# First graph layer of a four-layer network: one-hots built by ScalarE, message parts added in TensorE's sums, earlier record loads

## The chip, the cores and the metric

One core of one Trainium2 chip. The metric is the device time of the whole kernel in microseconds (us), the median of several runs. All four layers and their preparation are one program; the change touches the first layer's loop ("the product phase") and a few lines around it.

## What is computed

A node table `x` (6250 nodes x 64) passes through four graph layers over the same 200,000 edges, each followed by an addition and a layer norm. The change is in the first one:

```python
x0, x1 = x[:, :16], x[:, 16:].reshape(-1, 16, 3)          # of the edge's source node
w00, w01, w10, w11 = (silu(edge_attr @ w1 + b1) @ w2 + b2).reshape(-1, 4, 16, 16)
out0 = alpha * (einsum('eu,e,euw->ew', x0, sh0, w00) + einsum('eui,ei,euw->ew', x1, sh1, w11) / SQRT3)
out1 = alpha * (einsum('eu,ei,euw->ewi', x0, sh1, w01) + einsum('eui,e,euw->ewi', x1, sh0, w10)) / SQRT3
msgs = concatenate([out0, out1.reshape(-1, 48)], axis=1)
agg  = segment_sum(msgs, dst)
```

`sh0`, `sh1` are the edge's four harmonics. A message has 64 numbers: 16 in `out0`, 48 in `out1`.

## The kernel before

**Records.** The scatter phase (L269) writes one record of 112 numbers per edge to `rec_a` in HBM, sorted by blocks of destination nodes: the hidden activations in bf16 parts, `sh`, the source node (`R_SRC`) and the destination's lane within its chunk of 128 nodes (`R_LANE`).

**The product phase** (`product_phase`, L667) goes over `NB` = 104 blocks of `BT` = 16 tiles of 128 edges. Buffers `rec`, `hot`, `feat`, `xg` are double (index `q`), `msg` and `red` are single. Each engine has its own program, and semaphores tie them together:

- SP (L719 and on) loads records: `load(it, q)` waits until VectorE has released the buffer (`rec_used`), then issues the DMA. While blocks remain whose second record must be scattered (the first 100), SP then waits for the 16 scatters of this block (`rcb_sent`) and loads their source `rcb` (L728).
- GpSimd, called POOL (`one`, L733 and on), waits for the records, copies indices (L738 to L740), gathers 16 x 128 rows of `x` by indirect DMA (L743), makes the six factors `feat` (L752 to L759), and issues 16 indirect scatters to `rec_b` (L765).
- ScalarE (ACT) copies transposed hidden activations out of PSUM, once per four tiles (L785).
- TensorE (PE) makes the per-edge weights `p_rad` of each tile by four matmuls of 512 bf16 columns (`tile`, L809), in three PSUM buffers, and transposes the records four tiles at a time (L799, L801). Its `body` ends with the first three tiles of the next block, then waits for `msg_done`, then sums the block's messages into `p_sum`: 16 float32 matmuls `hot` x `msg` of 64 columns (L834). Only then comes tile 3 of the next block.
- VectorE (DVE) multiplies weights by factors (L873, L875), reduces over the 16 inputs (L882), and at the block's end runs, in this order: `reduce` of tile 15, two map words read into registers (`chunks`, L653 to L655, which say where the eight group sums go), three operations that make `msg` (L914, L915, L918), the one-hots `hot` of the next block (`hots`, L866: 128 x 2048 comparisons), and the next block's tiles 0, 1, 2 and on. The addition of `p_sum` to `acc` (L927, eight small ones) begins after the products of tile 2; the first waits for `sum_done`. The products of tile 3 come right behind it.

So PE's queue holds the order: first tiles of block b+1, sums of b, tile 3 of b+1; and DVE's holds: end of b, tiles 0 to 2 of b+1, first addition of b, tile 3 of b+1.

Of the kernel before, what the change touches and what calls it, by code (L numbers as in the profile page):

```python
# [13 lines left out]
P = 128  # L14
# [254 lines left out]
def scatter_phase(nc, g, ea_t, ea4, type64, w1, b1, w_comp, rec_a):  # L269

    with ExitStack() as ctx:
# [36 lines left out]
        ready = sem("s_ready")  # L308
        chain_s = sem("s_chain")
        typed = sem("typed")  # L310
        hots = sem("hots")
        edges_done = sem("edges_done")
        deg_done = sem("deg_done")
        acted = sem("acted")
        split = sem("split")
        turn = sem("s_turn")
# [350 lines left out]
def product_phase(nc, g, x, w2, b2, rec_a, stage_b, rec_b, acc):  # L667
# [6 lines left out]
    with ExitStack() as ctx:  # L674
# [18 lines left out]
        red = sb("red", [P, BT, 96])  # L693
        msg = sb("msg", [P, BT, D])
# [8 lines left out]
                                     "rec_used", "w_done", "turn", "chain", "pool_chain", "feat_done", "w_split", "w_stacked", "added"))  # L703
        block = ctx.enter_context(nc.Block())
# [3 lines left out]
        def _(sp):  # L708
# [7 lines left out]
            def load(it, q):  # L716
                b = it * 2 + q
                sp.wait_ge(rec_used, b + 1)
                sp.dma_start(rec[q][:, :, :].rearrange("p (n k) r -> p n (k r)", k=2),  # L719
                             ra[:, bass.ds(b * BG, BG), :]).then_inc(rec_in[q], 16)  # L720

            for q in range(2):
                sp.dma_start(rcb[q][:, :, :], stage_b[:, q * BT:(q + 1) * BT, :]).then_inc(rcb_in[q], 16)
            with sp.Fori(0, SB // 2 - 1) as it:
                for q in range(2):
                    load(it, q)
                    sp.wait_ge(rcb_sent[q], it * (16 * BT) + 16 * BT)
                    sp.dma_start(rcb[q][:, :, :], stage_b[:, bass.ds((it * 2 + (q + 2)) * BT, BT), :]).then_inc(rcb_in[q], 16)  # L728
            with sp.Fori(SB // 2 - 1, NB // 2) as it:
                for q in range(2):  # L730
                    load(it, q)
        @block.gpsimd
        def _(pool):  # L733
            ch = Chain(pool, pc)
            def one(it, q, scattering):
# [17 lines left out]
                ch.step(pool.tensor_tensor(f[:, :, 0, :], x0, bc(sh0, [P, BT, MUL]), ALU.mult))  # L753
                ch.step(pool.tensor_copy(f[:, :, 2, :], x0))
# [3 lines left out]
                ch.do(pool.tensor_tensor(f[:, :, 1, :], v4[:, :, :, 0], v4[:, :, :, 1], ALU.add))  # L758
                ch.do(pool.tensor_tensor(f[:, :, 1, :], f[:, :, 1, :], v4[:, :, :, 2], ALU.add))  # L759
# [19 lines left out]
        def _(act):  # L779
            act.sem_inc(kept, SEED)  # L780
            with act.Fori(0, NB) as b:
                for k in range(BT // 4):
                    hold(act, turn, turned, b * (BT // 4) + k + 1)
                    hold(act, turn, rad_done, b * BT + 4 * k + 1)
                    act.activation(hid_t[k % 2][0:K3, :, :, :], p_turn[:, :, :, :], ACT.Copy).then_inc(kept, 1)  # L785

        @block.tensor
        def _(pe):
            pe.wait_ge(w_done, 1)
            pe.wait_ge(w_stacked, 12 * 16)  # L790
            pe.sem_inc(added, 1)
            pe.sem_inc(rad_done, 5)
# [29 lines left out]
            def body(b, q, it, left):  # L822
# [18 lines left out]
        def _(dve):  # L841
# [7 lines left out]
            ch.step(dve.tensor_scalar(w2s[:, 0:MUL * MUL], w2s[:, 0:MUL * MUL], alpha, None, ALU.mult))  # L849
            ch.step(dve.tensor_scalar(w2s[:, MUL * MUL:COLS], w2s[:, MUL * MUL:COLS], alpha * 3.0 ** -0.5, None, ALU.mult))  # L850
# [8 lines left out]
            lane3 = bc(g["row"][:, :].unsqueeze(1), [P, BT, P])  # L859
# [19 lines left out]
            def reduce(j, behind):  # L879

                dve.wait_ge(chain_s, ch.n - behind)
                ch.step(dve.tensor_reduce(red[:, j, :], prod[j % 3][:, :, :], AX, ALU.add))  # L882
# [1215 lines left out]
```

## Time and profile before

| | |
|---|---|
| median of 3 runs | 21005.64 us (20965.97 to 21025.58) |
| the profiled execution's own time | 20999.39 us |
| its span, first to last instruction | 20997.5 us |
| granted TensorE clock, mean over the span | 0.652 of full |

Of the span, PE is busy 46%, DVE 74%, ACT 13%, POOL 62%. The page cuts the span into 40 slices of 525 us; the product phase runs from about 3295 to 9800 us, slices 6 to 18. A digit in a slice is the busy share in tenths. A timeline row reads: start in us, duration in us, engine, line, operation, output<-input, form, count, and in brackets the idle time of that engine just before with what ended it. A float32 matmul appears as two records, so the 16 sums of a block are 32 records, each with its own weight load.

### The profile page before, as it was taken

Reading aid. Unit: us, or ns where it says so; the run is one execution under the profiler, and the core shown is the slowest. Engines: PE = TensorE matmul, PEld = TensorE weight load, DVE = VectorE, ACT = ScalarE, POOL = GpSimd, SP = SyncE. Lnnn points to the kernel's source line nnn. Section 1 sums busy time; section 2 is a strip of 40 time slices with the busy share of each in tenths; the row PEclk is TensorE's granted clock in tenths of the full one; section 3 lists DMA queues with packets and bytes.
Section 4 is the critical chain, followed back from the end, with each engine's and each line's share of the span. In section 5 each row is a group of like instructions: output and inputs, shape, how many; then the busy total and the mean of one; then the engine's idle time right before and its main releaser. Section 6 shows DMA issues by size and latency. Waiting matters only on the chain. (4 is left out here: it accounts for less than half of the span.)

```text
span 20997.5 us, 207668 instructions
## 1 busy us (share of the span) xinstructions
PE 9692.8 (46%) x47565; PEld 6550.5 (31%) x47566; DVE 15524.9 (74%) x25713; ACT 2734.0 (13%) x6738; POOL 13093.3 (62%) x12678
## 2 busy tenths in 40 slices
PE   0333224655555555555777743332343433343443
PEld 0333222222222222222333333332333433343433
DVE  8555557999999999998888722222688887688887
ACT  0111100000000000000000000000233332233332
POOL 0788886666666666664777527774655653655653
PEclk9999996555555555555888855555555555555555
DMA  4333221111111111112111201114222222222222
GB/s 194 68 71 63 62 60 33 23 26 23 26 24 25 24 23 26 24 25 23 29 30 29 22 12 26 26 26 34 72 61 64 68 61 45 72 62 63 68 61 48
DMA packets 1151393, 956.47 MB, mean 46 GB/s; under 512 B 803963, under 2 KB 920315, under 8 KB 1150739
## 3 DMA queue, kind: packets, MB, share of 16 engines
q0 software_dynamic: 419904, 437.84, 12.3%
q1 hardware_dynamic: 730960, 512.22, 9.5%
q8 instruction: 253, 4.15, 0.1%
q14 instruction: 276, 2.26, 0.0%
HBM read 734.68 MB, written 210.63 MB: 45 GB/s over the span
## 5 line engine op out<-in xcount | busy, mean ns | idle before, releaser
L1539 POOL DMA_INDIRECT tail<-ball,h_idx x3328 | 3444.4, 1035 | 2802.9 <-DVEq L1864 1219.9
L809 PE MATMUL p_rad<-w_stack,hid_t 99*128 99x512 bf16 (+1 forms) x6656 | 2873.4, 588 | 2467.9 <-DVEq L908 1317.4
L1573 PE MATMUL h_sum<-head,h_hot 128*128 128x64 f32 x6656 | 1410.3, 410 | 3628.7 <-ACT head L1618 3273.9
L882 DVE TENSOR_REDUCE red<-prod 128x96 f32<-128x1536 f32 x1664 | 2904.0, 1745 | 3.5
L1573 PEld LDWEIGHTS h_sum<-head,h_hot 128*128 128x128 f32 x6656 | 1377.6, 320 | 3652.5 <-issue 3652.5
L345 POOL DMA_INDIRECT rec_a<-rec,slot x1600 | 2152.8, 1346 | 520.0 <-issue 492.6
L765 POOL DMA_INDIRECT rec_b<-l_rcb x1600 | 2077.2, 1298 | 570.6 <-issue 514.2
L1185 POOL DMA_INDIRECT l_xg<-h_tab,l_idx x1664 | 1570.0, 943 | 992.9 <-issue 492.3
L809 PEld LDWEIGHTS p_rad<-w_stack,hid_t 99*128 99x128 bf16 (+1 forms) x6656 | 776.3, 131 | 4215.2 <-issue 4159.3
L1007 POOL DMA_INDIRECT l_xg<-x_tab,l_idx x1664 | 1570.2, 944 | 662.2 <-issue 489.8
L743 POOL DMA_INDIRECT l_xg<-in_x,l_idx x1664 | 1577.7, 948 | 524.8 <-issue 475.5
L1021 PE MATMUL l_sum<-outer,l_hot 128*128 128x512 f32 x3328 | 1656.7, 662 | 534.6 <-DVEq L1066 534.6
L873 DVE TENSOR_TENSOR prod<-p_rad,feat 128x768 f32<-128x768 f32 x1664 | 1582.7, 951 | 84.0 <-PE p_rad L809 52.1
L875 DVE TENSOR_TENSOR prod<-p_rad,feat 128x768 f32<-128x768 f32 x1664 | 1579.6, 949 | 0.0
L365 PE MATMUL p_all<-w_all,kinds 97*125 97x40 f32 x3200 | 691.0, 409 | 1791.6 <-DVEq L478 1791.6
L664 DVE TENSOR_TENSOR acc_nodes<-acc_nodes,l_sum 128x64 f32 x832 | 183.7, 221 | 1646.2 <-PE l_sum L1197 1541.8
L1197 PE MATMUL l_sum<-l_xg,l_hot 128*128 128x64 f32 x3328 | 734.2, 422 | 1390.2 <-DMA l_xg<-h_tab,l_idx 1390.2
L365 PEld LDWEIGHTS p_all<-w_all,kinds 97*125 97x125 f32 x3200 | 679.4, 330 | 1803.4 <-issue 1803.4
L785 ACT ACTIVATE hid_t<-l_turn 96x1024 bf16<-96x1024 bf16 x416 | 424.4, 1020 | 6172.8 <-PE l_turn L801 6172.8
L1021 PEld LDWEIGHTS l_sum<-outer,l_hot 128*128 128x128 f32 x3328 | 698.6, 213 | 1492.1 <-issue 1492.1
L1197 PEld LDWEIGHTS l_sum<-l_xg,l_hot 128*128 128x128 f32 x3328 | 717.7, 332 | 1406.8 <-issue 1406.8
L1056 DVE TENSOR_TENSOR outer<-l_pcoef,l_xg 128x1024 f32<-128x1024 f32 x832 | 1015.5, 1221 | 96.4 <-DVE basis_sums L1048 45.2
(396 smaller groups left out, 18300.6 us busy)
## 6 DMA issues: line engine op xcount, KB each, us to landing
hot_t<-rows_l SPq DMA_DIRECT2D x208, 512.0 KB
rec_a<-fill SPq DMA_DIRECT2D x128, 728.0 KB, 19.6
l_rec<-rec_a SPq DMA_DIRECT2D x104, 896.0 KB, 4.8
rhot_t<-rows_r SPq DMA_DIRECT2D x208, 384.0 KB
tail<-ball,h_idx POOLq DMA_INDIRECT x3328, 2.5
t<-in_type SPq DMA_DIRECT2D x100, 500.0 KB
l_xg<-in_x,l_idx POOLq DMA_INDIRECT x1664, 2.4
l_xg<-x_tab,l_idx POOLq DMA_INDIRECT x1664, 2.4
```

Source lines behind the costliest of these rows:

```text
L345: pool.indirect_dma_start(rec_a[:, :], bass.IndirectOffsetOnAxis(ap=slot[q][:, j:j + 1], axis=0), rec[q][:, j, :], None).then_inc(sent[q], 16)
L743: pool.indirect_dma_start(xg[q][:, j, :], None, x[:, :], bass.IndirectOffsetOnAxis(ap=idx[q][:, j:j + 1], axis=0)).then_inc(gathered[q], 16)
L765: pool.indirect_dma_start(rec_b[:, :], bass.IndirectOffsetOnAxis(ap=rcb[q][:, j, 3:4].bitcast(U32), axis=0), rcb[q][:, j, :], None).then_i ...
L809: ins = pe.matmul(p_rad[j % 3][:, h * 512:(h + 1) * 512], hid_t[j // 4 % 2][0:K3 + 3 * (1 - i), j % 4, i, :], w_stack[i][0:K3 + 3 * (1 - i ...
L873: ch.step(dve.tensor_tensor(o[:, 0:48, :].rearrange("p (a w) u -> p a w u", a=3), w[:, 0:3], bc(f[:, j, 0:3, :].unsqueeze(2), [P, 3, MUL, ...
L875: ch.step(dve.tensor_tensor(o[:, 48:96, :].rearrange("p (w i) u -> p w i u", i=3), bc(w[:, 3].unsqueeze(2), [P, MUL, 3, MUL]), bc(f[:, j, ...
L882: ch.step(dve.tensor_reduce(red[:, j, :], prod[j % 3][:, :, :], AX, ALU.add))
L1007: pool.indirect_dma_start(xg[u][:, j, :], None, table[:, :], bass.IndirectOffsetOnAxis(ap=idx[u][:, j:j + 1], axis=0)).then_inc(gathered[u ...
L1021: ins = pe.matmul(p_sum[k % 4][:, :], hot[q][:, 2 * k + j, :], outer[k % 3][:, j, :, :].rearrange("p b d -> p (b d)"), start=(j == 0), sto ...
L1185: pool.indirect_dma_start(xg[u][:, j, :], None, table[:, :], bass.IndirectOffsetOnAxis(ap=idx[u][:, j:j + 1], axis=0)).then_inc(gathered[u ...
L1539: pool.indirect_dma_start(tg[q][:, j, :], None, table[:, :], bass.IndirectOffsetOnAxis(ap=idx[q][:, j:j + 1], axis=0)).then_inc(gathered[q ...
L1573: ins = pe.matmul(p_sum[u % 2][:, j % BT // 2, :], hot[j // HP8 % 3][:, j % HP8, :], hg[:, j, 0:D], start=(j % 2 == 0), stop=(j % 2 == 1))
```

## The change

Five things in the product phase: (1) `hots` moves to ScalarE, as 16 activations |lane - row| and one activation relu(1 - that), placed between its second and third copy of a block; SP's load now also waits for it. (2) The two map words are read behind tiles 14 and 15 instead of behind the last reduce. (3) `red` is double, the weights' order is changed, and what was added by L918 is now a second matmul: per tile one of 64 columns from `red` and one of 48 columns from `msg` into columns 16 to 63 of the same sum; the small addition of 16 columns stays on DVE, behind the multiplication. (4) SP issues the load of a buffer's next block before it waits for this block's scatters. (5) Nine semaphores of the scatter phase are taken from the shared pool and cleared behind it by one more small block.

```diff
@@ scatter_phase
-        ready = sem("s_ready")
...
-        turn = sem("s_turn")
+        again = shared(g, ["h_" + n for n in ("row_ready", "chain", "picked", "hot_done", "taken", "sum_done", "relu_done", "scaled", "turn")])
+        ready, chain_s, typed, hots, edges_done, deg_done, acted, split, turn = again
+        ctx.callback(clear_shared, nc, again)
@@ product_phase
-        red = sb("red", [P, BT, 96])
-        msg = sb("msg", [P, BT, D])
+        red = [sb(f"red{q}", [P, BT, 96]) for q in range(2)]
+        msg = sb("msg", [P, BT, 3 * MUL])
@@ sync
                 sp.wait_ge(rec_used, b + 1)
+                sp.wait_ge(hot_done, b + 1)
...
+            for q in range(2):
+                load(0, q)
             with sp.Fori(0, SB // 2 - 1) as it:
                 for q in range(2):
-                    load(it, q)
+                    load(it + 1, q)
                     sp.wait_ge(rcb_sent[q], it * (16 * BT) + 16 * BT)
...
-            with sp.Fori(SB // 2 - 1, NB // 2) as it:
+            with sp.Fori(SB // 2, NB // 2) as it:
@@ scalar
+            def hots(b, q, it):
+                hold(act, turn, rec_in[q], it * 16 + 16)
+                hold(act, turn, sum_done, b + 1)
+                for j in range(BT):
+                    ins = act.activation(hot[q][:, j, :], g["row"][:, :], ACT.Abs, scale=-1.0, bias=rec[q][:, j, R_LANE:R_LANE + 1])
+                ins.then_inc(away, 1)
+                hold(act, turn, away, b + 1)
+                act.activation(hot[q][:, :, :], hot[q][:, :, :], ACT.Relu, scale=-1.0, bias=g["ones"][:, 0:1]).then_inc(hot_done, 1)
...
+                        if k == 1:
+                            hots(b, q, it)
@@ tensor
                 hold(pe, turn, msg_done, b + 1)
+                hold(pe, turn, hot_done, b + 1 + SEED)
                 hold(pe, turn, added, b + 1)
                 for j in range(BT):
-                    ins = pe.matmul(p_sum[:, j // 2, :], hot[q][:, j, :], msg[:, j, :], start=(j % 2 == 0), stop=(j % 2 == 1))
+                    pe.matmul(p_sum[:, j // 2, :], hot[q][:, j, :], red[q][:, j, 2 * MUL:6 * MUL], start=(j % 2 == 0), stop=False)
+                    ins = pe.matmul(p_sum[:, j // 2, MUL:D], hot[q][:, j, :], msg[:, j, :], start=False, stop=(j % 2 == 1))
@@ vector
-            def hots(q, trip):
-                dve.wait_ge(rec_in[q], trip * 16 + 16)
-                ch.step(dve.tensor_tensor(hot[q][:, :, :], lane3, bc(rec[q][:, :, R_LANE:R_LANE + 1], [P, BT, P]), ALU.is_equal))
...
+                    if j >= BT - BG // PACK:
+                        chunk.extend(chunks(dve, g["map"][0], b * (BG // PACK) + (j - (BT - BG // PACK))))
-                reduce(BT - 1, 0)
-                chunk = [c for w in range(BG // PACK) for c in chunks(dve, g["map"][0], b * (BG // PACK) + w)]
+                reduce(BT - 1, q, 0)
                 ch.sync()
...
-                ch.step(dve.tensor_tensor(msg[:, :, 0:MUL], red[:, :, 0:MUL], red[:, :, MUL:2 * MUL], ALU.add))
-                ch.do(dve.tensor_tensor(m1, bc(red[:, :, 32:48].unsqueeze(3), [P, BT, MUL, 3]),
-                                        bc(sh1.unsqueeze(2), [P, BT, MUL, 3]), ALU.mult))
+                ch.step(dve.tensor_tensor(m1, bc(red[q][:, :, MUL:2 * MUL].unsqueeze(3), [P, BT, MUL, 3]),
+                                          bc(sh1.unsqueeze(2), [P, BT, MUL, 3]), ALU.mult))
+                ch.do(dve.tensor_tensor(red[q][:, :, 2 * MUL:3 * MUL], red[q][:, :, 2 * MUL:3 * MUL], red[q][:, :, 0:MUL], ALU.add))
                 dve.sem_inc(rec_used, 1)
-                ch.do(dve.tensor_tensor(msg[:, :, MUL:D], msg[:, :, MUL:D], red[:, :, 48:96], ALU.add))
                 dve.sem_inc(msg_done, 1)
-                if left:
-                    hots(1 - q, it + q)
```

The order of the weights' four paths in `w2` and `b2` and of POOL's factors `feat` is changed to match; their scaling takes four operations of 256 columns instead of two.

## Rows read from the trace of the kernel before

**Rows 1.** The page: busy time, and VectorE's busy tenths in 40 slices.

```profile
PE 9692.8 (46%) x47565; PEld 6550.5 (31%) x47566; DVE 15524.9 (74%) x25713; ACT 2734.0 (13%) x6738; POOL 13093.3 (62%) x12678
...
DVE  8555557999999999998888722222688887688887
```

**Rows 2.** Groups of instructions by line, product phase, 3298 to 9806 us.

```profile
L882 DVE TENSOR_REDUCE red<-prod 128x96 f32<-128x1536 f32 x1664 | 2904.0, 1745 | 3.5
...
L873 DVE TENSOR_TENSOR prod<-p_rad,feat 128x768 f32<-128x768 f32 x1662 | 1580.8, 951 | 55.9 <-PE p_rad L809 52.1 <-POOLq L760 3.2 <-DVE red L882 0.3
...
L834 PE MATMUL l_sum<-msg,l_hot 128*128 128x64 f32 x3328 | 678.7, 398 | 233.9 <-DVEq L919 233.9
...
L866 DVE TENSOR_TENSOR l_hot<-row,l_rec 128x2048 f32<-128x2048 f32 x103 | 237.9, 2310 | 24.9 <-DVE msg L918 24.8
```

**Rows 3.** Timeline of VectorE over one block's end.

```profile
5037.70 3.53 DVE L882 TENSOR_REDUCE red<-prod 128x96 f32<-128x1536 f32 x2
5042.31 0.43 DVE L914 TENSOR_TENSOR msg<-red 128x256 f32<-128x256 f32 x1 [1.09 <-issue]
5042.66 1.55 DVE L915 TENSOR_TENSOR msg<-red,l_rec 128x768 f32<-128x768 f32 x1
5044.36 0.96 DVE L918 TENSOR_TENSOR msg<-msg,red 128x768 f32<-128x768 f32 x1
5045.56 2.29 DVE L866 TENSOR_TENSOR l_hot<-row,l_rec 128x2048 f32<-128x2048 f32 x1 [0.24 <-DVE msg L918]
5047.77 0.95 DVE L873 TENSOR_TENSOR prod<-p_rad,feat 128x768 f32<-128x768 f32 x1
...
5056.41 0.95 DVE L873 TENSOR_TENSOR prod<-p_rad,feat 128x768 f32<-128x768 f32 x1
```

**Rows 4.** Timeline of TensorE over the same stretch.

```profile
5037.99 1.87 PE L809 MATMUL p_rad<-w_stack,hid_t 99*128 99x512 bf16 x4 [7.44 <-DVEq L908]
...
5040.50 3.29 PE L809 MATMUL p_rad<-w_stack,hid_t 99*128 99x512 bf16 x8
5045.67 6.08 PE L834 MATMUL l_sum<-msg,l_hot 128*128 128x64 f32 x32 [1.88 <-DVEq L919]
5051.54 3.62 PE L809 MATMUL p_rad<-w_stack,hid_t 99*128 99x512 bf16 x8
```

**Rows 5.** TensorE by stretch: length, busy (count), granted clock, DMA share, GB/s.

```profile
5044.00:5045.00 1.00, 0.00 (x0) 1.00 0.00 0
...
5049.00:5050.00 1.00, 1.00 (x6) 0.50 0.12 3
```

**Rows 6.** Stretches of L834 only: PE busy, PEld busy, granted clock, DMA, GB/s.

```profile
4983.30:4985.30 2.00, 2.00 (x19) 2.00 (x19) 1.00 0.07 2
4986.00:4988.00 2.00, 2.00 (x11) 2.00 (x11) 0.50 0.06 2
```

**Rows 7.** Timeline of TensorE: float32 matmuls of 64, 128 and 32 columns.

```profile
3610.73 7.06 PE L834 MATMUL l_sum<-msg,l_hot 128*128 128x64 f32 x32 [3.00 <-DVEq L919]
...
12056.24 1.09 PE L1124 MATMUL b_turn<-ident,b_stage 128*128 128x128 f32 x4 [4.28 <-DMA basis_w<-in_wt]
...
14681.55 3.16 PE L631 MATMUL p_outh<-rel_t,turnedh 64*128 64x32 f32 x14 [1.18 <-ACT turnedh L638]
```

**Rows 8.** Timelines of POOL and of SP's queue, two blocks' starts.

```profile
5009.67 0.40 SPq L719 DMA_DIRECT2D l_rec<-rec_a  x1
...
5014.70 0.20 POOL L738 CAST l_idx<-l_rec 128x16 uint32<-128x16 f32 x1 [7.43 <-DMA l_rec<-rec_a]
...
5077.19 0.20 POOL L738 CAST l_idx<-l_rec 128x16 uint32<-128x16 f32 x1 [7.51 <-DMA l_rec<-rec_a]
```

**Rows 9.** ScalarE: timeline of its copies, and one 128 x 128 activation.

```profile
5040.98 1.02 ACT L785 ACTIVATE hid_t<-l_turn 96x1024 bf16<-96x1024 bf16 x1 [9.14 <-PE l_turn L801]
5056.29 1.02 ACT L785 ACTIVATE hid_t<-l_turn 96x1024 bf16<-96x1024 bf16 x1 [14.29 <-PE l_turn L801]
...
L991 ACT ACTIVATE l_row<-row x1: 281/281/281, 9843.5 to 9843.5; 128x128 f32<-128x128 f32 x1
```

More of the change, by code:

```diff
@@ L703, in product_phase @@
                                      "rec_used", "w_done", "turn", "chain", "pool_chain", "feat_done", "w_split", "w_stacked", "added"))
+        away, hot_done = sem("l0_away"), sem("l0_hot_done")
         block = ctx.enter_context(nc.Block())
@@ L752, in one @@
                 ch.step(pool.tensor_tensor(v4, x1, bc(sh1.unsqueeze(2), [P, BT, MUL, 3]), ALU.mult))
-                ch.step(pool.tensor_tensor(f[:, :, 0, :], x0, bc(sh0, [P, BT, MUL]), ALU.mult))
-                ch.step(pool.tensor_copy(f[:, :, 2, :], x0))
+                ch.step(pool.tensor_tensor(f[:, :, 2, :], x0, bc(sh0, [P, BT, MUL]), ALU.mult))
+                ch.step(pool.tensor_copy(f[:, :, 1, :], x0))
                 for i in range(3):
@@ L757, in one @@
                 ch.sync()
-                ch.do(pool.tensor_tensor(f[:, :, 1, :], v4[:, :, :, 0], v4[:, :, :, 1], ALU.add))
-                ch.do(pool.tensor_tensor(f[:, :, 1, :], f[:, :, 1, :], v4[:, :, :, 2], ALU.add))
+                ch.do(pool.tensor_tensor(f[:, :, 0, :], v4[:, :, :, 0], v4[:, :, :, 1], ALU.add))
+                ch.do(pool.tensor_tensor(f[:, :, 0, :], f[:, :, 0, :], v4[:, :, :, 2], ALU.add))
                 pool.sem_inc(feat_done, 1)
@@ L780, in _ @@
             act.sem_inc(kept, SEED)
[L781 to L785, printed above, removed]
+            act.sem_inc(hot_done, SEED)
+            def hots(b, q, it):
[6 more added lines that the diff above has]
+                act.activation(hot[q][:, :, :], hot[q][:, :, :], ACT.Relu, scale=-1.0, bias=g["ones"][:, 0:1]).then_inc(hot_done, 1)
+            with act.Fori(0, NB // 2) as it:
+                for q in range(2):
+                    b = it * 2 + q
+                    for k in range(BT // 4):
+                        hold(act, turn, turned, b * (BT // 4) + k + 1)
+                        hold(act, turn, rad_done, b * BT + 4 * k + 1)
+                        act.activation(hid_t[k % 2][0:K3, :, :, :], p_turn[:, :, :, :], ACT.Copy).then_inc(kept, 1)
+                        if k == 1:
+                            hots(b, q, it)
         @block.tensor
@@ L791, in _ @@
             pe.sem_inc(added, 1)
+            pe.sem_inc(sum_done, SEED)
             pe.sem_inc(rad_done, 5)
@@ L848, in _ @@
             dve.wait_ge(loaded, 32)
-            ch.step(dve.tensor_scalar(w2s[:, 0:MUL * MUL], w2s[:, 0:MUL * MUL], alpha, None, ALU.mult))
-            ch.step(dve.tensor_scalar(w2s[:, MUL * MUL:COLS], w2s[:, MUL * MUL:COLS], alpha * 3.0 ** -0.5, None, ALU.mult))
+            for a in range(4):
+                path = slice(a * MUL * MUL, (a + 1) * MUL * MUL)
+                ch.step(dve.tensor_scalar(w2s[:, path], w2s[:, path], alpha if a == 2 else alpha * 3.0 ** -0.5, None, ALU.mult))
             ch.sync()
@@ L877, in products, with reduce @@
                                           bc(f[:, j, 3:6, :].unsqueeze(1), [P, MUL, 3, MUL]), ALU.mult))
-            def reduce(j, behind):
+            def reduce(j, q, behind):
                 dve.wait_ge(chain_s, ch.n - behind)
-                ch.step(dve.tensor_reduce(red[:, j, :], prod[j % 3][:, :, :], AX, ALU.add))
+                ch.step(dve.tensor_reduce(red[q][:, j, :], prod[j % 3][:, :, :], AX, ALU.add))
             EARLY = BG + 2
@@ L892, in first_tiles @@
                 dve.sem_inc(tile_done, 1)
-                reduce(0, 2)
+                reduce(0, q, 2)
                 dve.wait_ge(chain_s, ch.n - 1)
@@ L897, in first_tiles @@
                     products(b, q, j)
-                    reduce(j - 1, 2)
+                    reduce(j - 1, q, 2)
                     dve.wait_ge(chain_s, ch.n - 1)
@@ L2079 @@
         ("w1", a["L0_gnn_w1"]), ("b1", a["L0_gnn_b1"].reshape(1, HID)),
-        ("w2", a["L0_gnn_w2"].reshape(HID, 4, MUL, MUL)[:, [0, 3, 1, 2]].transpose(0, 1, 3, 2).reshape(HID, 4 * MUL * MUL)),
-        ("b2", a["L0_gnn_b2"].reshape(4, MUL, MUL)[[0, 3, 1, 2]].transpose(0, 2, 1).reshape(1, 4 * MUL * MUL)),
+        ("w2", a["L0_gnn_w2"].reshape(HID, 4, MUL, MUL)[:, [3, 1, 0, 2]].transpose(0, 1, 3, 2).reshape(HID, 4 * MUL * MUL)),
+        ("b2", a["L0_gnn_b2"].reshape(4, MUL, MUL)[[3, 1, 0, 2]].transpose(0, 2, 1).reshape(1, 4 * MUL * MUL)),
         ("wt", a["L1_gnn_weight"].reshape(NBAS * D, D)), ("w_comp", a["L1_gnn_w_comp"]), ("loop_w", a["L1_gnn_loop_weight"]),
```

16 lines of the change are left out of this document (4 added, 12 removed).

## The prediction

> **What bounds the kernel now.** I read the page first. Over the span no engine is full, but in slices 7 to 18 VectorE's digit is 9 [rows 1]; that is the product phase, some 6500 us. The groups of that stretch show why: 1664 tiles, each with a reduce of 1745 ns and two products of 950 ns, and the products waited in all only 55.9 us [rows 2]. VectorE bounds this phase, so a block's length is what its queue takes. I then read one block's end on VectorE as a timeline [rows 3] and the same stretch on TensorE [rows 4]. From the start of the last two reduces (5037.70) to the products of the next block's tile 3 (5056.41) pass 18.7 us, and every edit lies in there or is hidden. I take 5037.70 as zero below. The reduces end at 3.5, the products of tile 0 start at 10.1, those of tile 3 at 18.7. On TensorE the first three tiles run from 0.3 to 6.1, the engine idles 1.9 us waiting for the messages, the sums take 6.1 us, and tile 3 follows at 13.8, ready 1.9 later, long before it is wanted at 18.7. That spare time on TensorE, about 3 us, is what the change draws on.
>
> **VectorE's part of the sum.** What is left between the reduces' end (3.5) and tile 0: the step from a reduce's end to a dependent operation (0.15, as between L915's end 5044.21 and 5044.36), the multiplication (0.95 alone; 1.55 in the shown block, where POOL's arithmetic fell beside it), another step 0.15, the small addition (0.43, L914's time), and the semaphore and register work ahead of a product, which is hidden under L866 now and which I put at 0.45 (between 0.24, the gap ahead of L866, and 1.09, the gap of two map words) [rows 3]. Together 3.5 + 0.15 + 0.95 + 0.15 + 0.43 + 0.45 = 5.6. Tile 0 starts at 5.6 instead of 10.1: away are L918 (0.96), L866 (2.29) with its gap, the 1.09 of map words and part of the overlap with POOL. From tile 0 to tile 3 stay 8.64 us (5047.77 to 5056.41), so tile 3 is due at 14.3.
>
> The map words move under the reduces of tiles 13 and 14. They took 1.75 of the last reduce plus 1.09 of gap, 2.8 for two or 1.4 each, and the reduce that now covers each is 1.75 long [rows 3]. The wait of tile 15's products comes behind the first word, so I charge 0.3 per block; the bounds are 0 and the old 1.09. With it the stretch is 14.6, against 18.7: 4.1 us a block less, over 103 blocks 420 us, if TensorE keeps up.
>
> **TensorE's part.** The sums go from 32 records to 64. The question is what a record costs, and whether 48 columns are cheaper than 64. A run of records at the low clock gives it: 32 of 64 columns in 7.06 us, less the last one's modelled 0.42, is 0.214 each; 4 of 128 columns (1.09 - 0.42) / 3 = 0.22; 14 of 32 columns (3.16 - 0.40) / 13 = 0.21 [rows 7]. Columns between 32 and 128 don't matter, the weight load that goes with each record sets the pace, and 48 columns cost the same 0.214. At the full clock (2.4 GHz, 1.00) 19 records touch 2 us where 11 do at the half clock (1.2 GHz, 0.50) [rows 6]: less those already running, 0.112 against 0.214. So 64 records take 13.7 us at the half clock throughout and 7.2 at the full clock.
>
> The Trainium skill ("TensorE: Matmul & The Clock Gate", Part 2, step FILL) says that throughput is purely N cycles for N columns; by that rule the 48-column half would take three quarters of the other and the sums 12.0 and 6.3 us. The runs of 32 and of 128 columns disagree [rows 7], and I go by them.
>
> The sums can start when the first tiles end, at about 5.9 (a following record starts some 0.2 ahead of a modelled end, as 5051.54 against 5051.75) [rows 4]; the messages are there at 5.2, so the idle 1.9 us goes. Tile 3 needs 1.9 us at the half clock, 1.0 at the full one, and TensorE offers it at 5.9 + sums + that. It breaks even with today's block when that is 18.4 (18.7 less the 0.3 of map words): with 1.9 for the tile, sums of 10.6 us. So the sign hangs on the clock in the sums.
>
> What rows show of it: the clock stood at 1.00 in 5044 to 5045, just after the first tiles, though the engine was idle there [rows 5]; it is back at 0.50 by 5049, with the engine busy throughout the sums [rows 5]. In the block before it was 1.00 over the first 2 us of the sums and 0.50 afterwards [rows 6]. So dense bf16 tiles raise it, sums at the low clock don't raise it, and it fell after a stretch that held a gap of 1 to 2 us beside the sums. In the new order there is no gap: first tiles run into the sums. I take it that the level, once granted, mostly holds while matmuls follow each other without a gap; that is a choice, and rival C is its other side. Then tile 3 is offered at 5.9 + 7.2 + 1.0 = 14.1, just ahead of VectorE's 14.3. The added matmuls are hidden, with no spare left.
>
> The Trainium skill says (same page, Part 1, "What's actually happening") that the low clock is the default and activity releases it, so plain busyness through the sums should give the full clock. Here the trace disagrees in part: busy sums stayed at 0.50 [rows 5].
>
> **What is hidden.** ScalarE: 16 activations at 0.281 and one of 2048 elements, twice a copy's 1.02, make 6.5 us a block, behind the copy at 5040.98 and ahead of the one at 5056.29, with 14.3 us idle between [rows 9]; even 3 us more for function tables would fit. Their result is needed a block later. If this cover went, the third copy and so tile 8 would be late. The new wait for earlier sums (two blocks back) is long met. SP's new wait is for that ScalarE work, finished some 50 us before.
>
> POOL: its block is 62.5 us (5014.70 to 5077.19), the same as VectorE's, of which 7.5 is waiting for a record load that SP issues only behind the scatters and that lands 5 us later [rows 8]. With the load asked for when VectorE releases the buffer, POOL needs 55 us and stays ahead of VectorE's new 58.5. Without this part the other savings would have ended at POOL. SP's load of `rcb` now stands behind the wait for the next buffer; POOL needs it some 35 us later. POOL's factors are the same operations. Once only: four scaling operations for two, and one block of nine semaphore clears, 0 to 5 us, taken at 3.
>
> **Sum.** 20999.4 (profiled execution) - 420 + 3 = 20582. It lies 6 us under the median shown; and some blocks will lose the clock for a while, which I put at 0.15 us a block, 16 us. Forecast 20605.
>
> **Rivals.** A. As above, the full clock through nearly all sums, 20560 to 20700: 55%.
>
> B. The clock holds for part of the sums: about 4.5 us at 1.00 (40 records), then 24 at 0.214, 9.6 us; with 1.9 for tile 3 at 17.4 instead of 18.4: 1.0 us less, 20900; with 5.5 us held, 20800. 17%. For it: the clock fell inside the sums [rows 6].
>
> C. The slower side: the clock falls as it does now. The full level lasts some 2.5 us past the first tiles, as it did [rows 5, 6]: 22 records in it, 42 at 0.214, 11.5 us; tile 3 is offered at 19.3, VectorE stands 5 us at the first addition and the products of tile 3, and the block is 0.9 us longer: 21100. At the half clock throughout it is 21.5, 3.1 longer, 21320. The point is sums of 10.6 us. For it: busy sums did not bring the clock back [rows 5]. Against: the gap that stood before each fall. 15%.
>
> D. POOL binds: its load or its DMAs are later than I read, its block stays at 60.5 to 62.5 whatever VectorE does. 20800 to 21010. Against: the 7.5 us wait is plainly SP's order. 8%. The rest, 5%, is spread.
>
> By the skill's rule on activity (the page above) case A holds; by its column rule C would shrink to about today's time. Neither changes my chances.
>
> **How the numbers follow.** A measurement of this kernel tells 0.3%, 63 us, from no change. Faster: A, B, most of D and little else, 0.77; within: a piece of B and D, 0.08; slower: C, 0.15. The range goes from A's best, with the map words free and no POOL overlap (4.5 us a block, 20545), to 21000, which takes in B and D and leaves out C.
>
> **What the profile would show.** VectorE's gap ahead of the message operations gone, L866 and L918 gone, tile 0's products 5.6 us after the last two reduces start, and 64 sum records in 7 to 8 us at a granted clock of 1.00. A wait of VectorE's first addition or tile 3's products on TensorE is B or C, and its length times 103 is their price. A wait of POOL on the record load that is more than a few us while VectorE waits for `feat` is D. The forecast is wrong if the sums take over 9 us on average.

## The result and the profile after

| | before | changed |
|---|---|---|
| median, measured together, 4 runs each | 20992.87 us (20965.97 to 21025.58) | 20525.14 us (20519.97 to 20529.28) |
| ratio, 95% interval | | 0.9776, 0.9759 to 0.9793 |
| the profiled execution's own time | 20999.39 us | 20519.97 us |
| its span | 20997.5 us | 20518.2 us |
| granted TensorE clock, mean | 0.652 | 0.672 |

The change saves 468 us. The forecast said 20605, with 20545 as the low end. The time came out 80 us below the one and 20 below the other. The way it got there is the forecast's case A. Two kernels below each had one execution some 3 to 4% longer at a lower mean clock (21181.17 and 25926.24 us), and these two are left out of the ratios.

The page of the changed kernel, its busy sums and VectorE's and the clock's slices:

```profile
PE 9519.9 (46%) x50893; PEld 6556.5 (32%) x50894; DVE 15148.0 (74%) x25507; ACT 3428.6 (17%) x8506; POOL 12880.1 (63%) x12678
...
DVE  8545557999999999998888422222788887788887
...
PEclk9999997666666666667888655555555555555555
```

VectorE works 377 us less than before, ScalarE 695 us more; VectorE's digit is still 9 in the product phase, so it still bounds that phase [rows 1]. The clock's digits there are 6, where the kernel before has 5 in nearly all of them.

VectorE's timeline over one block's end, the stretch that answers to [rows 3]:

```profile
5027.43 3.53 DVE L894 TENSOR_REDUCE red<-prod 128x96 f32<-128x1536 f32 x2
5030.99 0.96 DVE L928 TENSOR_TENSOR msg<-red,l_rec 128x768 f32<-128x768 f32 x1
5031.87 0.42 DVE L930 TENSOR_TENSOR red<-red 128x256 f32<-128x256 f32 x1
5032.64 0.96 DVE L885 TENSOR_TENSOR prod<-p_rad,feat 128x768 f32<-128x768 f32 x1 [0.35 <-DVE red L930]
...
5041.15 0.21 DVE L938 TENSOR_TENSOR acc_nodes<-acc_nodes,l_sum 128x64 f32 x1
5041.47 0.96 DVE L885 TENSOR_TENSOR prod<-p_rad,feat 128x768 f32<-128x768 f32 x1
```

With 5027.43 as zero, tile 0 starts at 5.2 (10.1 before) and tile 3 at 14.0 (18.7 before). L866, L918 and the gap of the map words are gone. TensorE over the same stretch, its timeline and then its granted clock (length of the stretch, busy, clock, DMA share, GB/s):

```profile
5030.23 3.26 PE L824 MATMUL p_rad<-w_stack,hid_t 99*128 99x512 bf16 x8
5033.32 0.33 PE L850 MATMUL l_sum<-red,l_hot 128*128 128x64 f32 x2
...
5040.40 1.90 PE L824 MATMUL p_rad<-w_stack,hid_t 99*128 99x512 bf16 x8
```

```profile
5032.00:5033.00 1.00, 1.00 (x4) 0.51 0.03 1
5033.00:5034.00 1.00, 1.00 (x9) 1.00 0.37 49
...
5039.00:5040.00 1.00, 1.00 (x12) 1.00 0.00 0
```

The clock rises as the first tiles end, about 0.3 us before the sums (0.51 is the mean of the microsecond before 5033). The sums follow without a gap, and 64 records take 7.08 us (5033.32 to 5040.40) at 1.00. The 32 records of before took 5.9 us in the block shown (5045.67 to 5051.54), with the clock at 0.50 for most of it [rows 4, 5].

The table gives means over the 103 blocks, from the same rows of every block: the start of the two last reduces, of tile 0's and tile 3's products, and of the sums. The length of the sums is counted from their first record to the first matmul of tile 3, here and below.

| us per block | last reduces to tile 0 | tile 0 to tile 3 | tile 3 to the next last reduces | block | length of the sums |
|---|---|---|---|---|---|
| before | 10.01 | 8.64 | 43.90 | 62.55 | 6.3 |
| changed | 5.26 | 8.73 | 44.04 | 58.02 | 7.08 |

A block is 4.53 us shorter, 467 us over 103 blocks. The rest of the program differs by 13 us between the two profiled executions (14555 and 14542 us). The other kernels profiled on chips of this speed leave that rest as it is, and it takes 14534 to 14568 us in them.

ScalarE and POOL, one block of the changed kernel, one timeline each:

```profile
5031.63 4.77 ACT L786 ACTIVATE l_hot<-row,l_rec 128x128 f32<-128x128 f32 x16
5036.53 2.00 ACT L789 ACTIVATE l_hot<-l_hot,ones 128x2048 f32<-128x2048 f32 x1
5043.02 1.02 ACT L797 ACTIVATE hid_t<-l_turn 96x1024 bf16<-96x1024 bf16 x1 [4.49 <-PE l_turn L816]
```

```profile
5037.65 0.20 POOL L736 CAST l_idx<-l_rec 128x16 uint32<-128x16 f32 x1 [4.66 <-DMA l_rec<-rec_a]
```

ScalarE's new work takes 6.9 us and leaves 4.5 us idle before its next copy. POOL still waits 4.7 us for records in this block, and no wait of VectorE on POOL is found in the phase.

### The profile page after: what moved, and what is told of

The parts are those of the page before. It is cut to its first block and busy times, and to the rows that moved or that the text cites. A ratio compares the mean times of both kernels' runs of the same rounds, so it can differ in the third digit from the quotient of the medians.

```text
span 20518.2 us, 216572 instructions
## 1 busy us (share of the span) xinstructions
PE 9519.9 (46%) x50893; PEld 6556.5 (32%) x50894; DVE 15148.0 (74%) x25507; ACT 3428.6 (17%) x8506; POOL 12880.1 (63%) x12678
## 5 line engine op out<-in xcount | busy, mean ns | idle before, releaser
L824 PE MATMUL p_rad<-w_stack,hid_t 99*128 99x512 bf16 (+1 forms) x6656 | 2673.4, 554 | 2388.0 <-DVEq L921 1332.4
L763 POOL DMA_INDIRECT rec_b<-l_rcb x1600 | 1923.7, 1202 | 570.6 <-issue 514.0
L824 PEld LDWEIGHTS p_rad<-w_stack,hid_t 99*128 99x128 bf16 (+1 forms) x6656 | 720.6, 123 | 4025.1 <-issue 3901.3
L885 DVE TENSOR_TENSOR prod<-p_rad,feat 128x768 f32<-128x768 f32 x1664 | 1579.7, 949 | 145.7 <-PE p_rad L824 52.1
```

Source lines behind the costliest of these rows:

```text
L763: pool.indirect_dma_start(rec_b[:, :], bass.IndirectOffsetOnAxis(ap=rcb[q][:, j, 3:4].bitcast(U32), axis=0), rcb[q][:, j, :], None).then_i ...
L824: ins = pe.matmul(p_rad[j % 3][:, h * 512:(h + 1) * 512], hid_t[j // 4 % 2][0:K3 + 3 * (1 - i), j % 4, i, :], w_stack[i][0:K3 + 3 * (1 - i ...
L885: ch.step(dve.tensor_tensor(o[:, 0:48, :].rearrange("p (a w) u -> p a w u", a=3), w[:, 0:3], bc(f[:, j, 0:3, :].unsqueeze(2), [P, 3, MUL, ...
```

## The experiments

Each kernel was measured beside the kernel before on the same chip. "The changed kernel" means its two measurements, 20525.14 and, as the first run below, 20540.38.

**The changed kernel again.** No edit.

> The changed kernel itself, unedited, as the base of the others of this call, since chips differ in the later layers. Every theory: its product phase takes 58.0 us a block, the sums 7.1 us at the full clock. On a chip like the first one 20.5 thousand us in all.

Measured 20540.38 us (20521.13 to 20541.06), ratio 0.9763 (0.9747 to 0.9779). A second measurement lies 15 us from the first. The kernel before varies more from chip to chip: measured beside these runs it took 20992.87, 21039.3, 21021.74 and 21021.52 us. So differences of a few tens of us between medians of different chips tell little, and the mean length of a block (58.03 us here, 58.02 in the first profile) is the finer measure; it stands beside each median below.

**Record loads late again.** SP's part of the change undone:

```diff
-            for q in range(2):
-                load(0, q)
...
-                    load(it + 1, q)
+                    load(it, q)
```

> The changed kernel with the record load back behind the wait for the scatters. In the changed kernel POOL's block is 58.0 us long and 4.7 of it is waiting for a record load, so its own work is 53.4; the late load adds the 7.5 us it cost before. Theory 1 (POOL becomes the bound): block 60.8 to 61, 2.8 us over 100 blocks, 270 to 300 us above the changed kernel, VectorE waits for feat. Rival (transfers were hidden anyway, VectorE alone bounds): no more than 20 us above it.

Measured 20839.76 us, ratio 0.9919 (0.9902 to 0.9935): 299 to 315 us slower than the changed kernel. VectorE's waits over the product phase (total us, times, longest), then POOL and SP at one block:

```profile
DVE prod L883 <- POOLq L756: 187.7, 67, 4.1
...
DVE acc_nodes L936 <- PE l_sum L849: 70.8, 22, 6.3
```

```profile
5038.80 0.20 POOL L734 CAST l_idx<-l_rec 128x16 uint32<-128x16 f32 x1 [7.46 <-DMA l_rec<-rec_a]
```

```profile
5032.94 0.27 SPq L724 DMA_DIRECT2D l_rcb<-stage_b  x1
5033.46 0.40 SPq L715 DMA_DIRECT2D l_rec<-rec_a  x1
```

The load of records is issued behind that of `rcb`, so behind the wait for scatters; POOL waits 7.5 us for it, and now VectorE waits for POOL's factors. The block is 61.0 us, which makes 309 us over the phase, where 270 to 300 were expected. The prediction's sentence that without this part the savings would end at POOL holds, with POOL's block at 61.0 and not 62.5. The 70.8 us are a second price: in 22 blocks the sums lost the clock and took 11.3 to 13.7 us. In 14 of them TensorE had idled 0.4 to 1.5 us before the sums; in the other 8 it had not idled, and the clock had not yet risen when they began.

**The early load alone**, in the kernel before, on two chips:

> The kernel before with the early record load alone. Theory 1: VectorE bounds there, so only its collision with POOL's arithmetic goes (the stretch from the last two reduces to tile 0 is 10.01 us on average and 9.48 in undisturbed blocks): 30 to 55 us below the kernel before. Rival a (POOL's 62.5 us block is what set the period): 100 us or more below it. Rival b: no difference.

> The kernel before with the early record load alone, on a chip whose later layers run at the first chip's pace. Theory 1: VectorE bounds there; only its collision with POOL's arithmetic goes, 10.01 to 9.48 us between the last two reduces and tile 0: 40 to 60 us below the kernel before. Rival: no difference, the collision was no cost of the whole.

The second is the one to read: 20942.68 us, ratio 0.9959 (0.9945 to 0.9973), 79 us faster than the kernel before, where 40 to 60 were expected. So the early load gives something by itself, where POOL was not the bound. The three message operations, as groups of lines over the product phase, first in the kernel before and then with the early load:

```profile
L915 DVE TENSOR_TENSOR msg<-red,l_rec 128x768 f32<-128x768 f32 x104 | 117.2, 1127 | 0.0
L918 DVE TENSOR_TENSOR msg<-msg,red 128x768 f32<-128x768 f32 x104 | 106.5, 1024 | 15.3
L914 DVE TENSOR_TENSOR msg<-red 128x256 f32<-128x256 f32 x104 | 68.3, 657 | 114.3 <-issue 114.3
```

```profile
L920 DVE TENSOR_TENSOR msg<-msg,red 128x768 f32<-128x768 f32 x104 | 99.6, 958 | 15.3
L917 DVE TENSOR_TENSOR msg<-red,l_rec 128x768 f32<-128x768 f32 x104 | 98.9, 951 | 0.0
L916 DVE TENSOR_TENSOR msg<-red 128x256 f32<-128x256 f32 x104 | 44.2, 425 | 114.6 <-issue 114.6
```

The same three operations take 292.0 us and 242.7 us: 49 us of the gain is their collision with POOL's arithmetic, which the earlier load moves away from them. The trace of before shows this block by block: L915 takes 1467 ns on average in the 36 blocks where POOL's arithmetic runs beside it, and 943 to 954 ns in the other 68. With the early load POOL's arithmetic runs beside none of the three. The block is 0.54 us shorter, 55 us in all; the other 24 are within what the rest of the program scatters. The Trainium skill ("GPSIMD Engine Reference", 1. Specifications) says that GpSimd shares its SBUF interfaces with VectorE, and that they contend where a VectorE instruction has two SBUF inputs. All three operations have two, and the rows agree: 1127 against 951 ns for one of them.

**One-hots back on VectorE.**

```diff
-                        if k == 1:
-                            hots(b, q, it)
...
                 dve.sem_inc(msg_done, 1)
+                if left:
+                    hots(1 - q, it + q)
```

> The changed kernel with the one-hots back on VectorE, behind msg_done. Theory 1 (VectorE's queue sets the block, TensorE's sums stay hidden): tile 0 starts 2.2 us later, 225 to 250 us above the changed kernel. Rival (TensorE's tile 3 already sets the pace at 14.0 us after the last two reduces start): the one-hots hide under the sums and the cost is under 60 us.

Measured 20793.23 us, ratio 0.9893 (0.9877 to 0.991): 253 to 268 us slower. The comparison's group of lines:

```profile
L881 DVE TENSOR_TENSOR l_hot<-row,l_rec 128x2048 f32<-128x2048 f32 x103 | 236.1, 2292 | 35.1 <-DVE red L933 35.1
```

Tile 0 starts 2.15 us later (7.41 against 5.26), 222 us, which is VectorE's queue alone. The block is 60.47, so 252 us over the phase, where 225 to 250 were expected. Most of the other 30 us are seven blocks whose sums took 13.5 us. VectorE's wait for them (total us, times, longest; the end of the phase left out), then TensorE and its clock in one of them:

```profile
DVE acc_nodes L943 <- PE l_sum L847: 28.6, 7, 4.1
```

```profile
5032.34 3.62 PE L821 MATMUL p_rad<-w_stack,hid_t 99*128 99x512 bf16 x8
5035.76 0.52 PE L846 MATMUL l_sum<-red,l_hot 128*128 128x64 f32 x2
```

```profile
5036.00:5037.00 1.00, 1.00 (x7) 0.50 0.59 177
```

TensorE did not idle before these sums, but the clock had not risen when they began, and it stayed at 0.50 to their end. So the absence of a gap is not enough: the clock must also have risen in time. Over all blocks the sums took 7.55 us on average instead of 7.08.

**The large addition back on VectorE**, one matmul per tile:

```diff
-                    pe.matmul(p_sum[:, j // 2, :], hot[q][:, j, :], red[q][:, j, 2 * MUL:6 * MUL], start=(j % 2 == 0), stop=False)
-                    ins = pe.matmul(p_sum[:, j // 2, MUL:D], hot[q][:, j, :], msg[:, j, :], start=False, stop=(j % 2 == 1))
+                    ins = pe.matmul(p_sum[:, j // 2, :], hot[q][:, j, :], red[q][:, j, 2 * MUL:6 * MUL], start=(j % 2 == 0), stop=(j % 2 == 1))
...
+                ch.do(dve.tensor_tensor(red[q][:, :, 3 * MUL:6 * MUL], red[q][:, :, 3 * MUL:6 * MUL], msg[:, :, :], ALU.add))
                 dve.sem_inc(msg_done, 1)
```

> The changed kernel with the 48-column parts added on VectorE again (one operation of 768 elements more) and one matmul of 64 columns a tile instead of two. Theory 1: 1.0 to 1.1 us a block more, 105 to 115 us above the changed kernel, since the second matmul was hidden. Rival (the second matmul costs VectorE waiting that this run gives back): under 60 us above it, or none.

Measured 20637.56 us, ratio 0.982 (0.9803 to 0.9836): 97 to 112 us slower, a block of 59.05 instead of 58.02. The block's difference makes 106 us, and 105 to 115 were expected. It is the 1.0 us of the addition, and the 32 added records cost nothing.

**Map words behind the last reduce again.**

```diff
-                    if j >= BT - BG // PACK:
-                        chunk.extend(chunks(dve, g["map"][0], b * (BG // PACK) + (j - (BT - BG // PACK))))
...
                 reduce(BT - 1, q, 0)
+                chunk = [c for w in range(BG // PACK) for c in chunks(dve, g["map"][0], b * (BG // PACK) + w)]
```

> The changed kernel with both map words read behind the last reduce. The gap there was 1.09 us before, and the words cost 0.12 now. Theory 1: 0.95 us a block, 95 to 105 us above the changed kernel. Rival (the register work overlaps in any place, the gap was something else): under 30 us.

Measured 21229.98 us, ratio 1.0098 (1.0081 to 1.0115). That is 690 to 705 us slower than the changed kernel, where some 100 were expected, and slower than the kernel before. VectorE's waits in the product phase, TensorE at one block, and its clock there:

```profile
DVE acc_nodes L937 <- PE l_sum L851: 468.6, 104, 14.6
DVE prod L885 <- PE p_rad L824: 204.0, 233, 1.4
DVE msg L927 <- issue: 114.4, 104, 1.4
```

```profile
5033.65 3.04 PE L824 MATMUL p_rad<-w_stack,hid_t 99*128 99x512 bf16 x8
5037.46 0.41 PE L850 MATMUL l_sum<-red,l_hot 128*128 128x64 f32 x2 [0.77 <-DVEq L931]
...
5049.37 3.61 PE L824 MATMUL p_rad<-w_stack,hid_t 99*128 99x512 bf16 x8
```

```profile
5038.00:5039.00 1.00, 1.00 (x11) 1.00 0.78 99
5039.00:5040.00 1.00, 1.00 (x9) 0.69 1.01 349
5040.00:5041.00 1.00, 1.00 (x6) 0.50 1.09 382
```

The messages come 0.8 us behind the first tiles, TensorE idles for 0.77 us (0.2 to 1.6 over the blocks, 0.77 also on average), and then the clock falls inside the sums and stays at 0.50: 64 records take 11.9 us here, 12.3 on average. No block kept the clock; in 16 of them the sums ran at 0.50 from the first record. Tile 3 is ready late, and VectorE waits for both: (468.6 - 14.6) + (204.0 - 52.1) + 114.4 = 720 us more than in the changed kernel, less about 13 that the words no longer cost ahead of tile 15, 707. The block is 64.81 us, 699 over the phase. This is rival C of the prediction, brought on by messages that come later.

**The same, with more work in the gap.** Three bf16 matmuls of 512 columns are put between the first tiles and the wait for messages; what they write is overwritten by the sums.

```diff
+                hold(pe, turn, added, b + 1)
+                if left:
+                    flat = p_sum[:, :, :].rearrange("p n d -> p (n d)")
+                    for i in range(3):
+                        pe.matmul(flat, hid_t[0][0:K3, 2, 1, :], w_stack[1][0:K3, 0:512], start=True, stop=True)
                 hold(pe, turn, msg_done, b + 1)
```

> The kernel with the map words read last, which came out 705 us above the changed kernel where its own 0.97 us a block makes 100, and three bf16 matmuls of 512 columns into the still free sum bank between the first tiles and the wait for the messages, so that TensorE has no gap there. Their results are overwritten. Theory 1 (a gap of 0.8 us cost the full clock, and with it 5 us a block): the sums are back at 7.1 to 7.5 us and the whole is 110 to 170 us above the changed kernel. Rival (the later messages themselves, or register work on VectorE, cost the 705): no better than 600 us above it.

Measured 20626.4 us, ratio 0.9803 (0.9786 to 0.9819): 604 us less, by work that is thrown away. TensorE and its clock at one block:

```profile
5000.44 3.04 PE L824 MATMUL p_rad<-w_stack,hid_t 99*128 99x512 bf16 x8
5003.32 0.81 PE L850 MATMUL l_sum<-w_stack,hid_t 96*128 96x512 bf16 x3
5004.09 0.41 PE L854 MATMUL l_sum<-red,l_hot 128*128 128x64 f32 x2
...
5011.25 1.90 PE L824 MATMUL p_rad<-w_stack,hid_t 99*128 99x512 bf16 x8
```

```profile
5004.00:5005.00 1.00, 1.00 (x10) 1.00 0.23 12
```

The sums start as late as in the run before (6.6 us after the last reduces' start) and take 7.1 us, at 1.00 in every block. What is left, 86 to 101 us (110 to 170 were expected), is VectorE's: a block of 58.89, so 0.87 longer, 90 us. So the map words are worth about 90 us by themselves, and the other 604 were the clock.

That the length of the idle gap decides is not shown. In 46 of the 103 blocks of this run TensorE still idles 0.2 to 0.8 us before the sums, and they keep the clock all the same; in the run before, idle times as short as these lost it. TensorE at another block, and its clock late in those sums:

```profile
4413.65 0.81 PE L850 MATMUL l_sum<-w_stack,hid_t 96*128 96x512 bf16 x3
4415.25 0.41 PE L854 MATMUL l_sum<-red,l_hot 128*128 128x64 f32 x2 [0.79 <-DVEq L935]
```

```profile
4421.00:4422.00 1.00, 1.00 (x12) 1.00 0.00 0
```

The three matmuls both add work and shorten the gap, and no run separates the two.

**A gap made without touching VectorE's work ahead of it.** TensorE also waits for a product of the next block before the sums, in a short and a longer form (the second waits for one tile more):

```diff
+                if left:
+                    hold(pe, turn, tile_done, (b + 1) * BT + 4)
```

> The changed kernel, TensorE also waits for the products of the next block's tile 0 before the sums, so that it idles about 1.2 us between first tiles and sums. Theory 1 (clock): the full clock is kept because matmuls follow without a gap; with the gap it is lost in part of the blocks, sums of 8 to 12 us, 300 to 600 us above the changed kernel. Rival (the clock would hold over such a gap): the sums stay 7.1 us and start 1.2 later, 110 to 140 us above it.

> As the short gap, but waiting for tile 1's products too: about 3 us idle before the sums. Theory 1 (clock): lost in nearly every block, sums of 11 to 13.7 us, 3 + 4 to 6.6 + 0.9 us a block, 800 to 1050 us above the changed kernel. Rival (the clock holds): 3 us a block, 290 to 330 us above it.

> The changed kernel with 1.2 us more of waiting on TensorE ahead of the sums. Theory 1 (the clock is lost over a gap of that length, as it was over 0.8 us with the map words read last): sums of 12 to 13.6 us that start at 7.1 to 7.4, tile 3 offered at 21 to 23, 7 to 9 us a block, 700 to 900 us above the changed kernel (20.54 thousand). Rival (the clock holds): 110 to 140 us above it.

On the chip of the main comparison's speed the short form took 21388.65 us, ratio 1.017 (1.0154 to 1.0186), 848 to 864 us slower than the changed kernel, within the 700 to 900 expected, with a block of 66.36. The sums start 1.6 us later than in the changed kernel, and the expected cost of that delay alone was 110 to 140. TensorE's clock around one such start (sums from 5012.11, behind 1.63 us idle):

```profile
5011.00:5012.00 1.00, 0.00 (x0) 1.00 0.61 127
5012.00:5013.00 1.00, 0.89 (x8) 1.00 1.02 335
5014.00:5015.00 1.00, 1.00 (x6) 0.50 0.34 98
```

Here the sums take 12.9 us on average. The runs of the first two expectations fell on another chip, where the kernel before takes 24924.75 us, because its later layers are slower there (with the early load alone the last reduces of the product phase start at 9876 us there and 9736 elsewhere, and the program ends at 24934 and 20921); they gave 26042.74 and 26475.64, ratios 1.0448 and 1.0624. Their sums took 13.1 us behind the short gap and 13.6 behind the longer one. The order is the same, but on that chip other waits of the first layer are disturbed too, so their sizes are not used. For the same reason the early load alone gave a ratio of 1.0011 (1.0002 to 1.0021) there, with the stretch from the last reduces to tile 0 at 9.48 us, just as on the other chip.

**Products first.** Tile 0's products are put ahead of the wait for the small addition, whose end is signalled behind them:

```diff
                 products(b, q, 0)
+                told()
                 products(b, q, 1)
...
-                ch.do(dve.tensor_tensor(red[q][:, :, 2 * MUL:3 * MUL], red[q][:, :, 2 * MUL:3 * MUL], red[q][:, :, 0:MUL], ALU.add))
-                dve.sem_inc(rec_used, 1)
-                dve.sem_inc(msg_done, 1)
+                ch.step(dve.tensor_tensor(red[q][:, :, 2 * MUL:3 * MUL], red[q][:, :, 2 * MUL:3 * MUL], red[q][:, :, 0:MUL], ALU.add))
...
+                def told():
+                    dve.wait_ge(chain_s, ch.n - (2 if left else 0))
+                    dve.sem_inc(rec_used, 1)
+                    dve.sem_inc(msg_done, 1)
```

> The changed kernel, VectorE issues tile 0's products before it waits for the small addition and signals the messages. It removes the 0.35 us gap ahead of tile 0. Theory 1 (no spare left on TensorE: tile 3 is ready 14.0 us after the last two reduces start, and products of tile 3 start then): less than 15 us below the changed kernel, VectorE's wait ahead of tile 3 grows by 0.35. Rival (VectorE alone bounds): 35 us below it.

> The changed kernel with tile 0's products issued ahead of the wait for the small addition; beside the changed kernel on the same chip. Tile 0 starts at 4.8 instead of 5.3 us after the last two reduces start. Theory 1 (TensorE offers tile 3 at 14.0, no spare left): 0 to 20 us below the changed kernel. Rival: the whole 0.48 us a block, 45 to 50 us below it.

The second, measured beside the changed kernel, took 20549.35 us, ratio 0.9763 (0.9743 to 0.9782): nothing gained, and the block is 58.02 us as in the changed kernel; 0 to 20 us had been expected. (On the chip with slower later layers it gave 25048.67, ratio 1.0052.) VectorE at one block:

```profile
5031.70 3.53 DVE L894 TENSOR_REDUCE red<-prod 128x96 f32<-128x1536 f32 x2
...
5036.47 0.95 DVE L885 TENSOR_TENSOR prod<-p_rad,feat 128x768 f32<-128x768 f32 x1
...
5045.75 0.96 DVE L885 TENSOR_TENSOR prod<-p_rad,feat 128x768 f32<-128x768 f32 x1 [0.52 <-PE p_rad L824]
```

Tile 0 starts 0.48 us earlier on average (4.78), and all of it comes back ahead of tile 3, which TensorE offers no earlier: it starts 14.0 us after the last reduces in both kernels. That is the "no spare left" of the prediction.

**Tile 3 between the halves of the sums**, with the products first. TensorE makes tile 3 of the next block after eight of the sixteen sums; VectorE's additions begin one tile later.

```diff
                 for j in range(BT):
+                    if left and j == 8:
+                        tile(b + 1, 3)
...
-                    add(j - 2)
+                    if j > 2:
+                        add(j - 3)
```

> As the one with the products first, and TensorE makes tile 3 between the two halves of the sums, while VectorE adds the sums one tile later. Theory 1: that takes TensorE's limit away, so the 0.48 us and the small wait ahead of tile 3 (0.12) are won: 45 to 70 us below the changed kernel. Rival (splitting the sums loses the clock or the tile comes later for another reason): no gain or a loss.

Measured 20498.05 us (20496.37 to 20507.31), ratio 0.9744 (0.9727 to 0.976): 42 us faster than the changed kernel beside it, a little short of the 45 expected at least. With tile 3 offered early, the 0.48 us of the products count (49 us). But in four blocks the clock had not risen when the sums began. The stretch of sums and tile 3 took 15.1 us there, where 7.9 is usual, and VectorE waited 13.3 us in all for them. The block is 57.70 us, which makes 34 us over the phase. TensorE at one block, where its clock reads 1.00 in the microseconds on both sides of the tile:

```profile
5036.23 1.03 PE L824 MATMUL p_rad<-w_stack,hid_t 99*128 99x512 bf16 x4
5037.10 0.33 PE L852 MATMUL l_sum<-red,l_hot 128*128 128x64 f32 x2
```

This is the fastest version of the study, ahead of both kernels.

## Why the prediction was right and where it was wrong

**The bound and the way out** were right: VectorE's queue sets the block, and the gain is what left that queue. Taking one part back at a time gave its price: one-hots 222 us of queue time, addition about 106, map words about 90, and each close to what its rows said beforehand. With the collision's 49 to 55 they make 467 to 473, where the phase became 467 shorter.

**TensorE's part** was right in its numbers: a record at 0.112 us at the full clock and 64 of them in 7.2 us (7.08 measured), sums from 5.9 (5.83 on average), tile 3 offered at 14.1 (its products start at 13.99, and it is what VectorE meets first when it becomes faster). The choice on which the sign hung, that the full level mostly holds while matmuls follow without a gap, held in every block of this kernel. From the other side, with messages that leave a mean gap of 0.8 us ahead of the sums, the same 64 records take 12.3 us, and 7.1 with three more matmuls there. As to columns, 32 records of 64 columns take 3.60 us when they stand alone (5004.42 to 5008.02 in the run with the addition on VectorE), so the 48-column ones of the changed kernel take 7.08 - 3.60 = 3.48, 0.109 each. By the Trainium skill's rule that throughput is purely N cycles ("TensorE: Matmul & The Clock Gate", Part 2, step FILL) they would take 2.7 us, an estimate (three quarters of 3.60). The same page ("Back-to-back issue gap") says that in a stream of weight loads and matmuls the spacing is set by both, and with that part of it the rows agree.

**Luck had a part in it.** The forecast did not ask when the clock rises. In the changed kernel it rises 0.2 to 0.5 us before the sums in each of the 103 blocks, in both profiles. In kernels whose blocks have another length it came too late in some blocks: with the one-hots on VectorE in 7, with the late load in 8, with tile 3 between the halves in 4. Busy sums did not raise it there, as the forecast had read from [rows 5]. Why the rise comes in time in every block of the changed kernel is open.

**The step that failed is the sum on VectorE**, whose terms were mostly a little too careful, and with it the low end of the range. The forecast was the shown median, 21005.64, less 401 us; the saving is 468.

- From the last reduces to tile 0 the forecast had 5.6; measured 5.26. The small addition does not wait for the multiplication: it starts 0.88 us after it, ahead of its end in the trace, where 0.95 + 0.15 were charged. The same could be read in [rows 3], where L915 starts at 5042.66 and L914 ends at 5042.74. The multiplication starts 0.03 us after the reduces' end, where 0.15 were charged. The gap ahead of tile 0 is 0.39 on average, not 0.45. Worth 35 us.
- Map words: 0.3 forecast; 0.13 measured, as the stretch from tile 14's to tile 15's products is 3.52 us instead of 3.39, once a block. Worth 18 us.
- From tile 0 to tile 3: 8.64 forecast, 8.73 measured. Tile 3 waits a tenth for TensorE. It takes 10 us back.
- The lost clock, 16 us: the sums took 7.08 us in every block, so nothing. With the one-hots on VectorE it was 29 us.
- Outside the phase 3 us were added; no run shows them, and they are smaller than the scatter.

Together 35 + 18 - 10 + 16 + 3 = 62 of the 67 us by which the saving was larger; the other 5 are rounding in the forecast's sum and scatter. The last 13 of the 80 us are no saving at all: the kernel before, measured together with the changed one, took 20992.87 us and not 21005.64.

The low end of the range took the best case of these terms (4.5 us a block, 464 us) from the same 21005.64 and left no room below. The block alone came to 4.53, which is 3 us, the added 3 us did not show, and the base was 13 us lower: 19 of the 20 us. A range whose likeliest case lies at its low end needs room there for the terms' sizes and for a scatter of some 15 us.

**Rivals.** D is shown as the cost that the early load avoids: without it POOL binds at 61.0 us. C lay nearer than its 15% suggested: the map words' 1.1 us on VectorE, or a wait of 1.6 us on TensorE, is all that separates the changed kernel from one slower than before. Some blocks losing the clock and others not appears in the runs with the late load, the one-hots and tile 3 between the halves. That the four edits depend on each other was told for POOL and the early load, and missed for the map words and the clock. The forecast costed the words at what VectorE saves, and did not ask what TensorE would do in the 0.8 us by which the messages came later if they stayed.

## What to carry to other kernels

When work moves from a full engine to one with spare time, write down when the other engine's inputs come relative to its previous burst: here messages 0.8 us too late would have cost 600 us of clock, and three matmuls thrown away bought it back. Look also at how long before the moved work the clock rises, over all blocks, since a change in the block's length can move it. Price each edit in the new arrangement and not in the old one, since one edit (map words, early load) may be what lets the others count. If a second engine then becomes the first thing met, reorder its queue before shortening the first one's: shortening alone gave nothing, both gave 42 us.

## What the runs showed of the hardware

- Busy float32 matmuls of 48 and 64 columns ran at a full clock that was granted before them for 7 us in every block of the changed kernel. At 0.50 they do not bring it back: in the run with the map words last the clock fell at 5039.4 and stayed at 0.50 to the end of the sums, 10 us later, and in the run with the one-hots on VectorE seven blocks of sums that began at 0.50 without a gap stayed there for 13.5 us.
- Idle time need not lower the clock at once: with 0.77 us of gap the first 1.9 us of the sums still ran at 1.00, and with a gap of 0.89 us the 32 sums of the run with the addition on VectorE (from 5004.42) ended in 3.6 us at 1.00. Their average is 5.1, and 56 of the 103 blocks did run partly or wholly at 0.50.
- POOL's arithmetic beside VectorE operations with two SBUF inputs made them longer: by 33 to 63% in the blocks where it fell beside them (1272 against 958 ns for L918 and 693 against 425 ns for L914, 1467 against 950 ns for L915, means over such blocks).
- ScalarE's activation of 128x128 numbers with a bias of its own per partition follows at 0.30 us each (4.77 us for 16).
- One chip took 24924.75 us for the kernel before instead of some 21000; with the early load alone, what follows the product phase took 3873 us longer there than on another chip. Sizes were compared only between runs beside the same kernel on chips of the same speed.
